# A four-layer decoder on one core: the exponential and the context matmuls of three sixteen-head attentions in two halves, with part of a projection between them

## The chip, the cores and the metric

The kernel runs on one core of a Trainium2 chip, as one launch. The metric is the device time in microseconds (us). The time before is 2404.22 us, the median of three runs (2397.91 to 2418.76).

## What is computed

`reference.py` is a decoder of four layers over 16 sequences of 128 tokens with 256 features. Every layer has an attention, a cross-attention and a feed-forward part, each followed by a residual sum and a layer norm. Three of these twelve sublayers have sixteen heads of 16 features each, and only they are changed: the cross-attention of layer 0 (`l0_xattn`), the attention inside the feed-forward part of layer 0 (`l0_ffn_attention`) and the cross-attention of layer 2 (`l2_xattn`). The last of them is, cut:

```python
q = split_heads(query @ Wq + bq)          # 16 heads of 16
k = split_heads(key @ Wk + bk)
v = split_heads(value @ Wv + bv)
scores = einsum('bhqd,bhkd->bhqk', q, k) / sqrt(16)
attn = softmax(scores, axis=-1)
ctx = einsum('bhqk,bhkd->bhqd', attn, v)
return merge_heads(ctx) @ Wo + bo
```

The first has a ReLU on q, k and v and no output projection. The second attends over the batch axis for each token position, so that a mask is laid over the scores ("masked" below).

## The kernel before

All twelve sublayers run one after the other, with a barrier of all engines behind each. The three attentions share the class `Heads16`. It makes 16 steps, one for each sequence, and a few behind them. PSUM is used as eight banks of 512 float32 columns.

A step k of `run_pe`, which fixes the order of TensorE's work, is this:

- `scores` of sequence k into banks 0 to 3: 16 matmuls (each two instructions, since float32 takes two) with 32 rows of the array each, four side by side as row tiles. VectorE then takes the maximum of each query and head out of them (L576, one `reduce_max` over 128x2048).
- `context` of sequence k-1 into bank 4 (L499): 16 matmuls, each 32 columns of the array wide, four side by side as column tiles. It waits for `exp_ready`, the exponential of sequence k-1.
- the `pieces(k)`: projections (`project` L170, `project_tokens` L179) and transposes that the next group of four sequences or the output needs. A piece fills one of the banks 5, 6, 7, in turn over all pieces (`bank`), and is copied out by ScalarE (q, k: L297, two instructions a piece) or VectorE (v, y). `keep_running` (L110) puts a few idle matmuls there in some steps that have no piece.
- four transposes of the negated maxima into bank 0 (L512), which wait for VectorE's L576; VectorE adds them to q (L586).
- four transposes of the context of sequence k-1 into bank 1 (L521); VectorE divides by the sum (L592, L594).
- `shifted` scores of sequence k, keys by queries, into banks 4 to 7, so they wait until the context and all pieces have been copied out. They wait for L586.

ScalarE's step copies the context out of bank 4 (L546), takes its pieces, and makes the exponential of banks 4 to 7 in one instruction of 128x2048 (L556) into `probs`, `[128, 4, 4, 128]` by row group r and round t. So context k-1 lies between `scores` k and the pieces of k, and starts when the whole exponential is done, while every later use of banks 4 to 7 needs the same. Head h = 4t + r sits in row group r, which is bank 4 + r of `shifted`, and in column group r of the context. The host lays the weights out in that order (`slots`, `side_by_side`).

The pieces of a step go by its place in a group of four: two x, two k, ("turned" x only from the third group on); two c, one q; two y, one q; two v, two h. `l0_xattn` has k, q and v alone. The steps for the last group have no k, q, v of a next one.

## Time and profile before

| | |
|---|---|
| runs, median (lowest to highest) | 2404.22 us (2397.91 to 2418.76) |
| the profiled execution | 2399.57 us |
| its span, first to last instruction | 2397.8 us |
| mean granted clock of TensorE | 0.939 |
| `l0_xattn`, first to last exponential | 214.3 to 350.2 us |
| `l0_ffn_attention`, the same | 402.5 to 550.4 us |
| `l2_xattn`, the same | 1288.9 to 1422.1 us |
| exponentials L556 in all | 48 of 1877 ns |

In the profile, PE is TensorE's matmuls, PEld its weight loads, DVE is VectorE, ACT ScalarE, POOL GpSimd. A row of the timeline is: start in us, duration in us, engine, line, operation, output<-inputs, shape, count; in square brackets stands how long the engine had been idle before it and what it waited for. Consecutive instructions of one kind are merged into one row.

### The profile page before, as it was taken

What the parts mean: (1) busy time and instruction counts of PE and PEld (TensorE: products, weight loads), DVE (VectorE), ACT (ScalarE), POOL (GpSimd) and SP (SyncE); (2) the same over time, 40 slices, a digit from 0 to 9 for tenths busy, and PEclk for the clock granted to TensorE, in tenths of its full rate; (3) what the DMA queues carried; (4) which work ended last, traced back from release to release, by engine and by line L of the source; (5) the groups of instructions that cost most, each with busy time, mean ns of one, the idle gap of its engine ahead of it and who ended that gap; (6) DMA issues with size and microseconds to landing.
All of it is one profiled execution on the core that took longest, in us unless ns stands there. A gap on an engine that the chain in (4) does not pass through costs nothing. (4 is left out here: it accounts for less than half of the span.)

```text
span 2397.8 us, 37176 instructions
## 1 busy us (share of the span) xinstructions
PE 2017.7 (84%) x14090; PEld 1441.2 (60%) x14107; DVE 1440.8 (60%) x2869; ACT 935.7 (39%) x1542; POOL 784.6 (33%) x555
## 2 busy tenths in 40 slices
PE   6998765883996796599877879998998989789998
PEld 5775553662895585599535655684343434355887
DVE  3885884567233567211474564235799999999333
ACT  3433423430111344233334421113675666655443
POOL 1221231225002111100313014005688798978200
PEclk9999987996898887799988999999999999999999
DMA  5217001002996110799100003492210110200000
GB/s 169 80 41 268 19 23 50 2 19 71 336 382 231 46 36 18 275 357 380 47 1 28 2 2 131 124 269 85 80 42 30 36 35 25 95 9 1 10 10 18
DMA packets 104721, 232.65 MB, mean 97 GB/s; under 512 B 10016, under 2 KB 77472, under 8 KB 95584
## 3 DMA queue, kind: packets, MB, share of 16 engines
q1 hardware_dynamic: 95808, 208.24, 24.7%
q0 software_dynamic: 7680, 20.98, 2.7%
q8 instruction: 114, 1.87, 0.3%
q10 hardware_dynamic: 1056, 1.05, 0.1%
q14 instruction: 63, 0.52, 0.1%
HBM read 174.27 MB, written 55.97 MB: 96 GB/s over the span
## 5 line engine op out<-in xcount | busy, mean ns | idle before, releaser
L4273 POOL TENSOR_TENSOR l_attn_ring<-l_attn_ring,l_attn_c_rows 128x1024 f32<-128x1024 f32 x128 | 301.7, 2357 | 77.2 <-DVE l_attn_ring L4085 77.2
L4085 DVE TENSOR_TENSOR_SCAN l_attn_ring<-bank,l_attn_ring 128x512 f32<-128x512 f32 x256 | 299.2, 1210 | 21.5 <-ACT bank L3889 17.0
L3645 PE MATMUL bank<-l_attn_ring,identity 128*128 128x512 f32 x512 | 244.8, 600 | 17.2 <-POOL l_attn_ring L4273 13.9
L3889 ACT ACTIVATE bank<-l_attn_step,l_attn_minus_exp_a_log 128x508 f32<-128x508 f32 x256 | 173.8, 685 | 156.7 <-DVE l_attn_ring L4085 155.9
L170 PE MATMUL bank<-x_features,weights 128*128 128x512 f32 x416 | 199.2, 618 | 14.8 <-ACT l_attn_silu_z L3803 4.9
L3645 PEld LDWEIGHTS bank<-l_attn_ring,identity 128*128 128x128 f32 x512 | 95.5, 192 | 124.4 <-issue 98.0
L4079 DVE TENSOR_TENSOR l_attn_ring<-l_attn_step_times_input,bank 128x1024 f32<-128x1024 f32 x128 | 153.4, 1198 | 1.8 <-issue 1.3
L576 DVE TENSOR_REDUCE negmax_slots<-bank 128x16 f32<-128x2048 f32 x48 | 109.8, 2288 | 60.7 <-PE bank L462 60.3
L170 PEld LDWEIGHTS bank<-x_features,weights 128*128 128x128 f32 x416 | 79.0, 196 | 106.2 <-issue 87.4
L179 PE MATMUL bank<-weights,x_features 128*128 128x256 f32 (+1 forms) x336 | 99.7, 452 | 8.1 <-ACT weights L3919 3.3
L556 ACT ACTIVATE l_xattn_probs<-bank 128x2048 f32<-128x2048 f32 x32 | 60.1, 1877 | 102.2 <-PE bank L462 102.2
L1874 ACT ACTIVATE l_attn_hidden<-bank,l_attn_tile_weights 128x128 f32<-128x128 f32 x176 | 50.2, 368 | 110.9 <-PE bank L170 110.9
L179 PEld LDWEIGHTS bank<-weights,x_features 128*128 128x128 f32 x336 | 66.4, 202 | 37.0 <-issue 23.4
L170 PE MATMUL bank<-l_attn_tile_xT,l_attn_tile_weights 128*128 128x128 f32 x704 | 83.9, 278 | 3.5 <-DMA l_attn_tile_weights<-l_ffn_experts 3.5
L170 PEld LDWEIGHTS bank<-l_attn_tile_xT,l_attn_tile_weights 128*128 128x128 f32 x704 | 83.6, 195 | 4.7 <-issue 3.6
L179 PE MATMUL bank<-l_attn_tile_weights,l_attn_hidden 128*128 128x256 f32 x352 | 79.5, 379 | 0.0
L170 PEld LDWEIGHTS bank<-l_ffn_experts_tile_xT,ffn_experts_tile_weights 128*128 128x128 f32 x592 | 71.7, 192 | 3.6 <-issue 1.8
L1878 ACT ACTIVATE l_ffn_experts_hidden<-bank 128x512 f32<-128x512 f32 x39 | 23.3, 597 | 129.4 <-PE bank L170 129.4
L170 PE MATMUL bank<-l_ffn_experts_tile_xT,ffn_experts_tile_weights 128*128 128x128 f32 x592 | 72.3, 275 | 0.9 <-issue 0.9
L289 POOL TENSOR_SCALAR x_tokens<-x_tokens,l_xattn_x_mean_var,l_xattn_x_rstd 128x256 f32<-128x256 f32 x24 | 34.1, 1427 | 115.5 <-DVEq L285 115.5
L3956 ACT ACTIVATE weights<-bank,weights 128x512 f32<-128x512 f32 x64 | 45.6, 713 | 63.0 <-PE bank L3699 61.7
L179 PEld LDWEIGHTS bank<-l_attn_tile_weights,l_attn_hidden 128*128 128x128 f32 x352 | 65.2, 190 | 8.0
(750 smaller groups left out, 4417.2 us busy)
## 6 DMA issues: line engine op xcount, KB each, us to landing
l_attn_tile_weights<-l_ffn_experts SPq DMA_DIRECT2D x22, 2180.0 KB, 9.7
ffn_experts_tile_weights<-l_ffn_experts_experts SPq DMA_DIRECT2D x37, 1024.0 KB, 8.2
expert_slots<-zeros SPq DMA_DIRECT2D x8, 2048.0 KB, 11.6
l_attn_c_rows<-state_outputs SPq DMA_DIRECT2D x64, 256.0 KB, 3.3
l_ffn_tile_weights<-l_ffn_experts SPq DMA_DIRECT2D x23, 512.0 KB, 4.7
expert_slots<-residual_sum SPq DMA_DIRECT2D x62, 128.0 KB, 8.4
expert_slots<-zeros SPq DMA_DIRECT2D x1, 5888.0 KB, 27.8
l_ffn_tile_x<-expert_slots SPq DMA_DIRECT2D x23, 256.0 KB, 4.3
```

Of the source, the lines that this page charges most:

```text
L170: mm = pe.matmul(out, w[:, f, m * P:(m + 1) * P], src[:, f, :], start=start and f == 0, stop=stop and f == k - 1)
L179: mm = pe.matmul(out, srcT[:, f, seq(b)], w[:, f, :], start=start and f == 0, stop=stop and f == k - 1)
L289: engine.tensor_scalar(out, src, self.mv[:, n, 0:1], self.rstd[:, n:n + 1], ALU.subtract, ALU.mult).then_inc(done, 1)
L556: nc.scalar.activation(self.probs[k % 2][:].rearrange("p r t q -> p r (t q)"), self.shifted, ACT.Exp, scale=self.scale).then_inc(self.exp_ ...
L576: nc.vector.reduce_max(slots[:, :, SHIFT_ROW].rearrange("p (t r) -> p r t", t=4), self.scores.rearrange("p r (t k) -> p r t k", t=4), AX_X ...
L1874: ins = net.nc.scalar.activation(self.hidden[t % 2][:, m, :], bank[:, i * self.tile:(i + 1) * self.tile], self.func, bias=self.b1(t, m))
L3645: mm = pe.matmul(net.banks[SUMS[j]][:], net.ident[:], ring[n % 4][:, j, :], start=s == 0, stop=s == STATES - 1)
L3889: nc.scalar.activation(by_seq(net.banks[DECAY[j]][:])[:, :, 1:], by_seq(dt[:, m, :])[:, :, 1:], ACT.Exp, scale=a[:, m * STATES + s:m * STA ...
L3956: nc.scalar.activation(full[n % 3], out[:], ACT.Relu, scale=by).then_inc(full_ready, 1)
L4079: tt(ring[n % 4][:], dtu[:, 2 * half_:2 * half_ + 2, :], net.banks[B_ROW[n % 2]][:].unsqueeze(1).broadcast_to([P, 2, T]), ALU.mult).then_i ...
L4085: nc.vector.tensor_tensor_scan(ring[n % 4][:, j, :], net.banks[DECAY[j]][:], ring[n % 4][:, j, :], 0.0, ALU.mult, ALU.add).then_inc(state_ ...
L4273: tt(ring[n % 4][:], ring[n % 4][:], c_row[:, n % STATES, :].unsqueeze(1).broadcast_to([P, 2, T]), ALU.mult).then_inc(out_ready, 1)
```

## The change

- `run_act` makes the exponential of a step with two instructions of 128x1024, the first over banks 4 and 5, the second over banks 6 and 7. Each counts up `exp_ready`.
- `run_pe` makes the context in two halves of eight heads (`context_half`), the first when the first exponential is done, the second when the second is. Both use all four column groups. For that the heads are laid out anew, by the host (`by_place`): heads 8c to 8c+7 lie in the row groups 2c and 2c+1.
- Between the halves stands what `between(k)` names: of a first piece k, q, v or y its first part (`project`: the first of two blocks of the contraction, `project_tokens`: the first of two sequences); of a first piece h, x or c the whole of it; nothing where there is none. The rest comes behind the second half.
- A step's pieces now take the banks 5, 6, 7 from bank 5 on in each step (`side`), so the first piece is in a bank that the first exponential has read. `last_there` names the piece that was in the same bank before.

Of the diff, the new signatures of `work` in `l0_ffn_attention` and `l2_xattn` are left out; they pass `parts` on as that of `l0_xattn` does.

```diff
--- before.py
+++ after.py
@@ -163,10 +163,10 @@
                 mm.then_inc(done, 1)
 
 
-def project(pe, out, w, src, m, start=True, stop=True):
+def project(pe, out, w, src, m, start=True, stop=True, of=None):
 
     k = w.shape[1]
-    for f in range(k):
+    for f in range(k) if of is None else of:
         mm = pe.matmul(out, w[:, f, m * P:(m + 1) * P], src[:, f, :], start=start and f == 0,
                        stop=stop and f == k - 1)
     return mm
@@ -388,6 +388,7 @@
 
     SIDE = (5, 6, 7)
     STEPS = SEQUENCES + 5
+    IN_PARTS, TURNED = "kqvy", "hxc"
 
     def __init__(self, net, sub, signals, masked, scale, first, pieces, by_act, steps=STEPS, fill={}, ahead=None):
         self.STEPS, self.ahead = steps, ahead
@@ -399,6 +400,10 @@
         order = list(first) + [p for k in range(self.STEPS) for p in pieces(k)]
         self.by_act = by_act
         self.number = {p: n for n, p in enumerate(order)}
+        self.side = {p: self.SIDE[i % 3] for ps in [list(first)] + [pieces(k) for k in range(self.STEPS)]
+                     for i, p in enumerate(ps)}
+        self.last_there = {p: max([m for m in range(n) if self.side[order[m]] == self.side[p]], default=-1)
+                           for n, p in enumerate(order)}
         self.act_upto, self.dve_upto = [], []
         for p in order:
             self.act_upto.append((self.act_upto or [0])[-1] + by_act(p))
@@ -438,7 +443,7 @@
         return slots_act(self.net, to, src, func, u, own, bias)
 
     def bank(self, name):
-        return self.net.banks[self.SIDE[self.number[name] % 3]]
+        return self.net.banks[self.side[name]]
 
     def wait_taken(self, engine, n):
 
@@ -464,15 +469,32 @@
                                skip_group_check=True, tile_position=(at, 0))
         return mm
 
+    def between(self, k):
+
+        names = self.pieces(k)
+        if names and names[0][0] in self.IN_PARTS:
+            return [(names[0], (1,))] + [(name, (0, 1)) for name in names[1:]], [(names[0], (0,))]
+        ahead = 1 if names and names[0][0] in self.TURNED else 0
+        return [(name, (0, 1)) for name in names[ahead:]], [(name, (0, 1)) for name in names[:ahead]]
+
     def run_pe(self, pe, work):
         net, done = self.net, 0
 
-        def do(name):
-            n = self.number[name]
-            if n >= 3:
-                self.wait_taken(pe, n - 3)
-            net.keep_running(pe, self.bank(name), self.fill.get(name, 0))
-            work(self.bank(name), *name).then_inc(self.filled, 1)
+        def do(name, parts=(0, 1)):
+            if 0 in parts:
+                self.wait_taken(pe, self.last_there[name])
+            mm = work(self.bank(name), *name, parts)
+            if 1 in parts:
+                mm.then_inc(self.filled, 1)
+
+        def context_half(n, c):
+            pe.wait_ge(self.exp_ready, 2 * n + c + 1)
+            for h in range(8 * c, 8 * c + 8):
+                at, t, r = SLOT * (h % 4), 2 * (h // 4 % 2) + h // 2 % 2, 2 * c + h % 2
+                mm = pe.matmul(self.ctxT[at:at + SLOT, seq(h // 4)], self.v1(n // NB, n % NB)[:, h, :],
+                               self.probs[n % 2][:, r, t, :], start=True, stop=True,
+                               skip_group_check=True, tile_position=(0, at))
+            return mm
 
         for name in self.first:
             do(name)
@@ -490,19 +512,18 @@
                                    net.mates_q, net.mates_k).then_inc(self.scores_ready, 1)
             if 1 <= k <= SEQUENCES:
                 n = k - 1
-                pe.wait_ge(self.exp_ready, n + 1)
                 if n % NB == 0 and ("v", n // NB, 1) in self.number:
                     self.wait_taken(pe, self.number["v", n // NB, 1])
-                for t in range(4):
-                    for r in range(4):
-                        at = SLOT * r
-                        mm = pe.matmul(self.ctxT[at:at + SLOT, seq(t)], self.v1(n // NB, n % NB)[:, 4 * t + r, :],
-                                       self.probs[n % 2][:, r, t, :], start=True, stop=True,
-                                       skip_group_check=True, tile_position=(0, at))
-                mm.then_inc(self.contextT_ready, 1)
-            for name in self.pieces(k):
-                do(name)
-                done += 1
+                context_half(n, 0)
+                behind, between = self.between(k)
+                for name, parts in between:
+                    do(name, parts)
+                context_half(n, 1).then_inc(self.contextT_ready, 1)
+            else:
+                behind = [(name, (0, 1)) for name in self.pieces(k)]
+            for name, parts in behind:
+                do(name, parts)
+            done += len(self.pieces(k))
             if ("max", k) in self.fill:
                 self.wait_taken(pe, done - 1)
                 net.keep_running(pe, net.banks[7], self.fill["max", k])
@@ -553,8 +574,9 @@
                 act.wait_ge(self.shifted_ready, k + 1)
                 if k >= 2:
                     act.wait_ge(self.contextT_ready, k - 1)
-                nc.scalar.activation(self.probs[k % 2][:].rearrange("p r t q -> p r (t q)"), self.shifted,
-                                     ACT.Exp, scale=self.scale).then_inc(self.exp_ready, 1)
+                for of in (slice(0, 2), slice(2, 4)):
+                    nc.scalar.activation(self.probs[k % 2][:, of, :, :].rearrange("p r t q -> p r (t q)"),
+                                         self.shifted[:, of, :], ACT.Exp, scale=self.scale).then_inc(self.exp_ready, 1)
 
     def run_dve(self, dve, chain, take, rest, between=None):
         net, nc = self.net, self.net.nc
@@ -1157,12 +1179,12 @@
             def _(pe):
                 pe.wait_ge(net.ready["l0_xattn"], 16)
 
-                def work(out, kind, g, i):
+                def work(out, kind, g, i, parts):
                     if kind == "k":
-                        return project(pe, out, wk, net.ctxT_all[:, g, :, :], i)
+                        return project(pe, out, wk, net.ctxT_all[:, g, :, :], i, of=parts)
                     if kind == "q":
-                        return project(pe, out, wq, net.xT_all[:, g, :, :], i)
-                    for b in (2 * i, 2 * i + 1):
+                        return project(pe, out, wq, net.xT_all[:, g, :, :], i, of=parts)
+                    for b in (2 * i + part for part in parts):
                         mm = project_tokens(pe, out[:, (b % 2) * D:(b % 2 + 1) * D], net.ctxT_all[:, g, :, :], b, wv)
                     return mm
 
...
@@ -1285,9 +1307,9 @@
                     if kind == "k":
                         if i == 0:
                             heads.wait_taken(pe, heads.number["h", g, 1])
-                        return project(pe, out, wk, xT, i)
+                        return project(pe, out, wk, xT, i, of=parts)
                     if kind == "q":
-                        return project(pe, out, wq, xT, i)
+                        return project(pe, out, wq, xT, i, of=parts)
                     if kind == "logits":
                         if g == 0:
                             pe.wait_ge(net.ready["l0_ffn_experts"], 16)
@@ -1300,7 +1322,7 @@
                         return route.count_pe(pe, out, of_group(g))
                     if kind == "y" and i == 0:
                         heads.wait_taken(pe, heads.number["c", g, 1])
-                    for b in (2 * i, 2 * i + 1):
+                    for b in (2 * i + part for part in parts):
                         to = out[:, (b % 2) * D:(b % 2 + 1) * D]
                         mm = project_tokens(pe, to, cT, b, wo) if kind == "y" else project_tokens(pe, to, xT, b, wv)
                     return mm
...
@@ -3038,12 +3060,12 @@
                         pe.wait_ge(heads.context_ready, NB * (g + 1))
                         return turn(out, heads.context, i)
                     if kind == "k":
-                        return project(pe, out, wk, net.ctxT_all[:, g, :, :], i)
+                        return project(pe, out, wk, net.ctxT_all[:, g, :, :], i, of=parts)
                     if kind == "q":
-                        return project(pe, out, wq, net.xT_all[:, g, :, :], i)
+                        return project(pe, out, wq, net.xT_all[:, g, :, :], i, of=parts)
                     if kind == "y" and i == 0:
                         heads.wait_taken(pe, heads.number["c", g, 1])
-                    for b in (2 * i, 2 * i + 1):
+                    for b in (2 * i + part for part in parts):
                         to = out[:, (b % 2) * D:(b % 2 + 1) * D]
                         if kind == "y":
                             mm = project_tokens(pe, to, cT, b, wo)
@@ -4614,9 +4636,17 @@
     return v.reshape(-1, P).T
 
 
+def by_place(a):
+
+    import numpy as np
+    heads = np.arange(NH).reshape(2, 2, 2, 2).transpose(1, 2, 0, 3).reshape(-1)
+    return a.reshape(*a.shape[:-1], NH, DH)[..., heads, :].reshape(a.shape)
+
+
 def slots(a, row=0.0):
 
     import numpy as np
+    a = by_place(a)
     out = np.zeros((*a.shape[:-1], 2, 2, 4, SLOT), a.dtype)
     heads = a.reshape(*a.shape[:-1], 2, 2, 4, DH)
     out[..., 0, :, 0:DH], out[..., 0, :, SHIFT_ROW] = heads[..., 0, :, :], row
@@ -4627,7 +4657,7 @@
 def side_by_side(a):
 
     import numpy as np
-    heads = a.reshape(*a.shape[:-1], 2, 2, 4, DH)
+    heads = by_place(a).reshape(*a.shape[:-1], 2, 2, 4, DH)
     return np.ascontiguousarray(np.swapaxes(heads, -3, -2)).reshape(*a.shape[:-1], D)
 
 
```

## Rows read from the trace of the kernel before

**Rows 1.** The page, busy time of each engine
```profile
PE 2017.7 (84%) x14090; PEld 1441.2 (60%) x14107; DVE 1440.8 (60%) x2869; ACT 935.7 (39%) x1542; POOL 784.6 (33%) x555
```

**Rows 2.** Who waited for whom, PE alone, of `l0_xattn`, `l0_ffn_attention`, `l2_xattn` (total us, times, longest)
```profile
PE bank L499 <- ACT l_xattn_probs L556: 16.4, 16, 2.0
PE bank L512 <- DVE negmax_slots L576: 8.2, 5, 2.1
...
PE bank L499 <- ACT l_ffn_attention_probs L556: 15.4, 16, 2.0
PE bank L512 <- DVE negmax_slots L576: 5.2, 1, 5.2
...
PE bank L499 <- ACT l_xattn_probs L556: 17.7, 16, 2.0
PE bank L512 <- DVE negmax_slots L576: 0.8, 2, 0.6
```

**Rows 3.** Timeline of one step of `l0_xattn` with two k pieces
```profile
238.93 1.07 PE L462 MATMUL bank<-l_xattn_k_slots,l_xattn_q_slots 32*128 32x128 f32 x32
239.17 1.88 ACT L556 ACTIVATE l_xattn_probs<-bank 128x2048 f32<-128x2048 f32 x1 [5.08 <-PE bank L462]
241.10 1.08 PE L499 MATMUL bank<-l_xattn_probs,values_and_one 128*32 128x128 f32 x32 [1.10 <-ACT l_xattn_probs L556]
242.11 3.70 PE L170 MATMUL bank<-ctx_features,weights 128*128 128x512 f32 x8
242.87 2.27 DVE L576 TENSOR_REDUCE negmax_slots<-bank 128x16 f32<-128x2048 f32 x1
245.65 0.60 PE L512 MATMUL bank<-identity,negmax_slots 128*128 128x128 f32 x4
247.64 1.17 PE L462 MATMUL bank<-l_xattn_q_slots,l_xattn_k_slots 32*128 32x128 f32 x32 [0.96 <-ACT l_xattn_k_slots L297]
```

**Rows 4.** Groups of instructions on ACT, each shape apart (busy us, mean ns)
```profile
L556 ACT ACTIVATE l_xattn_probs<-bank 128x2048 f32<-128x2048 f32 x32 | 60.1, 1877 | 102.2 <-PE bank L462 102.2
L1878 ACT ACTIVATE l_ffn_experts_hidden<-bank 128x512 f32<-128x512 f32 x39 | 23.3, 597 | 129.4 <-PE bank L170 129.4
L2378 ACT ACTIVATE l_attn_gate<-x_tokens 128x1024 f32<-128x1024 f32 x4 | 4.2, 1057 | 0.1
```

**Rows 5.** Timeline of another stage: whole-array transposes, then row tiles
```profile
74.57 0.60 PE L958 MATMUL bank<-identity,residual_sum 128*128 128x128 f32 x4
...
75.10 1.15 PE L926 MATMUL bank<-l_attn_qk,weights 32*128 32x256 f32 x16
```

**Rows 6.** Timeline: a masked step with one q piece, and the wait for the exponential
```profile
404.49 2.29 DVE L576 TENSOR_REDUCE negmax_slots<-bank 128x16 f32<-128x2048 f32 x1
407.27 0.60 PE L512 MATMUL bank<-identity,negmax_slots 128*128 128x128 f32 x4
...
513.02 1.08 PE L499 MATMUL bank<-l_ffn_attention_probs,values_and_one 128*32 128x128 f32 x32 [0.90 <-ACT l_ffn_attention_probs L556]
```

**Rows 7.** Timeline of a step of `l0_xattn` that waits for VectorE (PE, then DVE)
```profile
263.46 0.66 PE L512 MATMUL bank<-identity,negmax_slots 128*128 128x128 f32 x4 [1.86 <-DVE negmax_slots L576]
264.90 2.09 PE L462 MATMUL bank<-l_xattn_q_slots,l_xattn_k_slots 32*128 32x128 f32 x32 [0.34 <-DVE l_xattn_q_slots L586]
...
261.12 2.29 DVE L576 TENSOR_REDUCE negmax_slots<-bank 128x16 f32<-128x2048 f32 x1
```

**Rows 8.** Timeline of the last step of `l0_xattn`
```profile
348.35 1.88 ACT L556 ACTIVATE l_xattn_probs<-bank 128x2048 f32<-128x2048 f32 x1 [4.42 <-PE bank L462]
350.28 1.93 PE L499 MATMUL bank<-l_xattn_probs,l_xattn_values_and_one 128*32 128x128 f32 x32 [2.00 <-ACT l_xattn_probs L556]
```

**Rows 9.** Busy time and granted clock of the three stages (us busy, counts, PEclk, DMA share)
```profile
214.30:354.00 139.70, 106.00 (x1709) 79.81 (x1707) 117.02 (x161) 54.36 (x55) 39.16 (x28) 0.94 0.23 79
402.50:552.00 149.50, 119.91 (x1927) 93.06 (x1920) 94.82 (x203) 58.56 (x61) 43.86 (x33) 0.97 0.03 9
1288.90:1424.00 135.10, 106.66 (x1759) 83.34 (x1752) 73.49 (x129) 56.05 (x56) 15.76 (x13) 0.98 0.01 2
```

4 lines of the change are left out of this document (2 added, 2 removed).

## The prediction

> **What bounds the kernel now.** I read the page first: TensorE is busy for 84% of the span, the other engines for 60% or less [rows 1]. So TensorE's idle time is what a change of order can win, and only in the three stages that it touches. They last some 140, 150 and 135 us [rows 9], 425 of 2398 us.
>
> Next the waits of TensorE in these stages. The context matmuls (L499) wait for the exponential (L556) 16 times in each, 16.4, 15.4 and 17.7 us in all: 49.5 us, or 1.03 us at each of 48 steps. The maxima's transposes (L512) wait for VectorE's reduction (L576) 8 times, 14.2 us in all [rows 2].
>
> Then the timeline of a step. `scores` end at 238.93 + 1.07 = 240.00. The exponential started at 239.17 and ends at 241.05, and the context starts at 241.10. Between them TensorE has nothing, for 1.10 us [rows 3]. In the masked stage the mask's matmuls fill 0.2 us of it, and 0.9 is left [rows 6]. From there pieces, transposes and the `shifted` scores follow without a wait that doesn't move with the pieces: the last take of a piece, or L586, ends 1 us after the transposes start. So the chain of a step is exponential, context, pieces, transposes, L586 or L297, `shifted`, exponential. It has a second strand, `scores` to L576 to the transposes.
>
> **The change, part by part.**
>
> *The exponential in two.* Not in the trace is a 128x1024 one from PSUM. Of the same engine 128x512 from PSUM takes 597 ns and 128x2048 takes 1877 [rows 4], that is 0.833 ns per column. So 1024 columns take 597 + 427 = 1024 ns. The 1057 ns of a 128x1024 with its input in SBUF is near it. The second half ends at 2.05 us after the start, 0.17 later than now. That costs nothing while TensorE works on a piece until then.
>
> *The first context half* can start 1.02 + 0.05 = 1.07 us after the start of the exponential, not 1.93. `scores` have ended by then (0.83; masked 1.04, so perhaps 0.03 later). So 0.86 us of the idle time goes.
>
> *TensorE's work is the same, but the form of the matmuls changes twice more in a step*: column tiles, whole array, column tiles, whole array, where there was one such change. From tiles to the whole array: the 32 context instructions start 0.026 us apart ((1.08 - 0.27) / 31, each lasting 0.27), so they need 0.84, and the projection starts 1.01 after them: 0.17. Its 8 instructions then take 3.54 until the transposes, against 8 x 0.43 = 3.44: 0.10 more [rows 3]. Together 0.27. From the whole array to tiles I have only the row tiles of another stage: four transposes 0.109 apart should be through at 75.01, and the tiles start at 75.10: 0.09 [rows 5]. So the two extra changes cost 0.36 us. The lower bound is 0, if the weight loads go ahead beside the running matmuls. The upper is 0.62, if both changes also expose the whole of a load and of a last matmul's tail (0.11 + 0.16, 0.19 + 0.16 from the durations in the same rows). I take 0.36, because the rows show these very changes or the nearest ones.
>
> The Trainium skill speaks against this edit ("TensorEngine Tiling (Array Packing)", Key Properties): to change the tiling mode drains TensorE. It gives no price. Its page "TensorE: Matmul & The Clock Gate" (Single matmul latency) has 398 cycles beside the columns for a matmul that nothing overlaps. By that a drain would be 166 ns at 2.4 GHz, two of them 0.33, and the sum 1 us better than mine.
>
> *What a step gains*: 0.86 - 0.36 = 0.50 us, if there is work for between the halves and the second half isn't reached early. First half and change last 0.42 + 0.27, part of a k, q, v or y piece 0.86 (two instructions of 0.43, or four of 0.22), a whole x, c or h piece 0.44. So the second half is reached 2.2 us after the start at the earliest, behind the second exponential's 2.10.
>
> *Where it is lost.* A step whose transposes wait for L576 gains nothing. They do so at 8 steps [rows 2], at one of which the reduction starts only at 261.12, behind VectorE's layer norm, and TensorE stands for 1.86 us [rows 7]. Going through all 48 steps, I find three more that are held in this way or another: by the reduction's end within 0.1 us, by VectorE's two takes of v behind a late reduction, and by `scores` that run at half clock. These 11 are steps 5, 9 and 11 to 14 of `l0_xattn` (counting from 0), 10 and 14 of `l0_ffn_attention`, 0, 2 and 14 of `l2_xattn` (its 0 is the one with the slow `scores`). In the last step of each stage there is no new sequence. The other 34 have a slack of 0.4 us or more. One of the tightest is the q step where L576 ends at 406.78 and the transposes start at 407.27 [rows 6]; it loses nothing, since ScalarE's take of q ends later than L586 there.
>
> *The last steps.* Here the context runs at half clock, 1.93 us after a wait of 2.00 [rows 8]. With halves of 0.97 the first runs beside the second exponential, and the second ends at 2.10 + 0.97 = 3.07 after the start, not at 3.86. That is 0.8 us in `l0_xattn`, and perhaps 0.5 and 0.6 in the two stages where an x piece stands between: 1.9 us.
>
> *Banks, copies, the other queues.* The first piece goes into bank 5 in every step, but all pieces were already waited for ahead of `shifted`, so no wait is added. The context's copy (L546) comes some 0.3 us later or at the same time as now; it is followed by takes that come 0.5 earlier and still start after it. No DMA is added or moved; SP's and POOL's queues keep their order. Behind the stages the barriers pass every gain on.
>
> *The sum*: 34 x 0.50 + 1.9 = 18.9 us, 19. Against the profiled execution's own time, 2399.6, that is 2380.6. The median of the runs is 4.6 us above that execution, and I set the gain against the median: 2404.2 - 19 = **2385 us**, 0.8% faster. With 0.62 for the changes it is 34 x 0.24 + 1.9 = 10, or 2394. With 0 it is 34 x 0.86 + 1.9 = 31, less some 3 where the slack is below 0.86: 28, or 2376.
>
> **The rivals.**
>
> *The changes of form are hidden*: 2376. For it: TensorE loads weights ahead in long streams. Against it: the gap of 0.17 behind each context.
>
> *VectorE takes over in more steps.* L576 needs 2.29 us each time and VectorE is busy for 117 of 140 us in `l0_xattn` [rows 9]. A step that gets shorter brings its norms and sums nearer to the next reduction. In the 9 steps of that stage that I count on, half of the gain may go, and as much in the masked stage if the routing joins in: 9 us less, 2394. Against it: the slack that I found in each step.
>
> *The gain is given back at the ends of the stages*, say because weights that are being fetched arrive no earlier: 2404. Against it: DMA is nearly idle in two of the stages [rows 9].
>
> *Slower: the clock.* The mean granted clock is 0.94 to 0.98 in the stages [rows 9], and the half clock (1.2 of 2.4 GHz) shows around the steps where TensorE waits for VectorE: behind the 1.86 us of idleness `scores` take 2.09 us, not 1.17 [rows 7]. The change turns the short wait for the exponential into a longer one for L576 in just these 11 steps. A whole step at half clock costs 0.9 for each of three groups of tiles and 1.7 for a q piece, some 4 us. From 5 such steps on the gain is gone. If all 11 get there, it is 44 - 19 = 25 us slower: 2429. Against it: the idle time of a whole step stays the same or gets less.
>
> **How the numbers follow.** The forecast 0.57 (its own range 2378 to 2392), hidden changes 0.13, VectorE 0.15, given back 0.07, slower 0.08. The range reaches from 5 us below 2376 to just above 2404, 2371 to 2405, and leaves out the slower case and a little on both sides. A change of less than 1% (24 us) can't be told from none here, since the three runs of before lie 21 us apart; 1% faster is below 2380.2. By the cases: 0.12 of the hidden changes and 0.2 of the forecast make 0.32 faster; slower by over 1% is the clock's 0.08; the rest, 0.60, is within 1%.
>
> **What would show it.** In the profile after: L556 96 times at 1.02 us; the first context half 1.07 us after the first exponential, with an idle time of 0.2 before it; the second half with no wait for the exponential in 34 steps, and 0.2 to 0.3 us between its last instruction and the projection. The sum of TensorE's waits on L556 falls from 49 us to some 12. The three stages get shorter by 5.3, 7.0 and 6.6 us. The waits of L512 on L576 grow from 14 us to some 20. I'm wrong about the changes of form if a step with a q piece gets shorter by 0.2 or by 0.8 rather than 0.5; wrong about VectorE if L512 waits at more than 12 steps; wrong about the clock if a stage's granted clock falls below 0.9.

## The result, and the profile after

The changed kernel takes 2389.45 us (median of 12 runs, 2379.76 to 2397.83), the kernel before in the same session 2407.88 (12 runs, 2397.91 to 2418.76): a ratio of 0.9924, with an interval of 0.9906 to 0.9943. In a later session it was 2393.33 against 2403.75: 0.9946 [0.9924, 0.9968]. So it is 0.5 to 0.8% faster, 13 to 18 us by the ratios and 10 to 18 by the medians. 2385 was predicted, 19 less than the median known then; that median rose by 3.7 us with more runs. Of the first kernel under "The experiments" one run took 4230.23 us, the nine others 2412.56 to 2424.67; its ratio leaves that run out.

The profiled execution of after takes 2390.27 us (span 2388.5), the one of before 2399.57. Its busy line, beside [rows 1]:

```profile
PE 2038.9 (85%) x14090; PEld 1438.0 (60%) x14107; DVE 1441.8 (60%) x2869; ACT 938.4 (39%) x1590; POOL 783.7 (33%) x555
```

The same 14090 matmuls, and 48 more instructions on ScalarE: the second exponentials. The groups of the exponentials (busy us, mean ns), beside [rows 4]:

```profile
L578 ACT ACTIVATE l_xattn_probs<-bank 128x1024 f32<-128x1024 f32 x64 | 62.1, 1021 | 97.9 <-PE bank L467 97.9
```

1021 ns each; 1024 was worked out. TensorE's waits in `l0_xattn`, `l0_ffn_attention` and `l2_xattn` (total us, times, longest), beside [rows 2]; L494 is the context, L578 the exponential, L533 the maxima's transposes, L598 the reduction:

```profile
PE bank L533 <- DVE negmax_slots L598: 10.8, 6, 2.6
PE bank L494 <- ACT l_xattn_probs L578: 5.7, 18, 1.1
...
PE bank L533 <- DVE negmax_slots L598: 5.8, 1, 5.8
...
PE bank L494 <- ACT l_ffn_attention_probs L578: 1.4, 2, 1.2
...
PE bank L494 <- ACT l_xattn_probs L578: 5.3, 17, 1.1
...
PE bank L533 <- DVE negmax_slots L598: 1.6, 2, 1.0
```

The waits for the exponential fell from 49.5 to 12.4 us (12 predicted), those for the reduction rose from 14.2 to 18.2 (20 predicted), at 9 places rather than 8. The step of [rows 3] is now this (start, duration):

```profile
236.62 1.94 ACT L578 ACTIVATE l_xattn_probs<-bank 128x1024 f32<-128x1024 f32 x2 [4.22 <-PE bank L467]
237.69 0.64 PE L494 MATMUL bank<-l_xattn_probs,values_and_one 128*32 128x128 f32 x16 [0.25 <-ACT l_xattn_probs L578]
238.27 1.12 PE L170 MATMUL bank<-ctx_features,weights 128*128 128x512 f32 x2
239.32 0.64 PE L494 MATMUL bank<-l_xattn_probs,values_and_one 128*32 128x128 f32 x16
239.90 2.84 PE L170 MATMUL bank<-ctx_features,weights 128*128 128x512 f32 x6
240.31 2.28 DVE L598 TENSOR_REDUCE negmax_slots<-bank 128x16 f32<-128x2048 f32 x1
242.64 0.66 PE L533 MATMUL bank<-identity,negmax_slots 128*128 128x128 f32 x4
244.48 1.17 PE L467 MATMUL bank<-l_xattn_q_slots,l_xattn_k_slots 32*128 32x128 f32 x32 [0.74 <-ACT l_xattn_k_slots L297]
```

The first half starts 1.07 us after the exponential, as predicted, where the whole context started at 1.93. The idle time before it is 0.25, not 1.10. The second half waits for nothing. The transposes start 6.02 after the exponential (6.48 before) and `shifted` 7.86 after it (8.47 before). The reduction ends at 242.59 here, so it is VectorE that sets the transposes' 242.64, and by 0.1 us at most (in the third kernel below, with no such wait, they start 2.68 after the same six matmuls do; here it is 2.74).

The steps of this kernel repeat so exactly that they measure better than the total. I call a step the time from one (first) exponential to the next. In two executions of before the 34 steps that the prediction counted on agree to 0.01 us on the mean. Here they are, with the rest of the span beside them (us; "three last steps" is the sum over the stages of the time from the last step's first exponential to its context's transposes):

```
                                     before   before   after    after    after
                                              again             again    timed
34 steps, against before                  -      0.0   -17.0    -16.4    -16.4
the 11 other steps                     99.7     98.2    98.3    100.8    101.3
three last steps, exponential to
  the context's transposes             14.6     13.7    10.5     11.0     11.0
last exponential of l0_ffn_attention
  to the first of l2_xattn            740.4    736.7   750.8    738.0    756.9
span                                 2397.8   2397.2  2388.5   2379.8   2397.2
```

The 34 steps gained 0.48 to 0.50 us each. The fourth line, a stretch that the change doesn't touch, lies between 737 and 757 us. In the profiled execution of after it took back 10.5 of the 22.5 us that the first three lines had gained, and the rest of the span another 2.7, so the spans are only 9.3 apart.

### The profile page after: what moved, and what is told of

Same layout as the page of the kernel before. It is cut to its first block and busy times, and to the rows that moved or that the text cites. A ratio compares the mean times of both kernels' runs of the same rounds, so it can differ in the third digit from the quotient of the medians.

```text
span 2388.5 us, 37231 instructions
## 1 busy us (share of the span) xinstructions
PE 2038.9 (85%) x14090; PEld 1438.0 (60%) x14107; DVE 1441.8 (60%) x2869; ACT 938.4 (39%) x1590; POOL 783.7 (33%) x555
## 5 line engine op out<-in xcount | busy, mean ns | idle before, releaser
L170 PE MATMUL bank<-x_features,weights 128*128 128x512 f32 x416 | 204.5, 627 | 17.0 <-ACT l_attn_silu_z L3825 4.9
L598 DVE TENSOR_REDUCE negmax_slots<-bank 128x16 f32<-128x2048 f32 x48 | 109.8, 2287 | 59.6 <-PE bank L467 59.1
L578 ACT ACTIVATE l_xattn_probs<-bank 128x1024 f32<-128x1024 f32 x64 | 62.1, 1021 | 97.9 <-PE bank L467 97.9
```

Source lines behind the costliest of these rows:

```text
L170: mm = pe.matmul(out, w[:, f, m * P:(m + 1) * P], src[:, f, :], start=start and f == 0, stop=stop and f == k - 1)
L578: nc.scalar.activation(self.probs[k % 2][:, of, :, :].rearrange("p r t q -> p r (t q)"), self.shifted[:, of, :], ACT.Exp, scale=self.scale ...
L598: nc.vector.reduce_max(slots[:, :, SHIFT_ROW].rearrange("p (t r) -> p r t", t=4), self.scores.rearrange("p r (t k) -> p r t k", t=4), AX_X ...
```

## The experiments

**Taking the change apart.** Three kernels, and the one with a whole piece between that follows them, were compared with the kernel before at 2412.37 us (median). After each measured time stand its ratio to the kernel before with the 95% interval, and the mean change of the 34 steps against before. The first has the two exponentials and two halves of the context, but both halves wait for the second exponential, and nothing stands between them:

```diff
-            pe.wait_ge(self.exp_ready, 2 * n + c + 1)
+            pe.wait_ge(self.exp_ready, 2 * n + 2)
...
-                behind, between = self.between(k)
+                behind, between = [(name, (0, 1)) for name in self.pieces(k)], []
```

> The changed kernel with the exponential still in two instructions, but the whole context behind both of them and nothing between its halves. What is left of the change is the second instruction's fixed cost and the new places of heads and banks. Mine: the context starts 2.10 us after the first exponential instead of 1.93, so a step that TensorE's chain sets is 0.17 us longer than before: 34 such steps make 6 us, ratio to the kernel before 1.002 to 1.003. Rival, the extra ACT instruction is free or the new places gain something: step lengths as before or shorter, ratio 1.000 or less. A loss of over 0.3 us a step would mean that the two instructions cost more than the rows of before made likely.

Measured: 2415.39 us (median of all ten runs), 1.0016 [0.9993, 1.0039]; 0.085 a step (0.06 in most, 0.15 in every fourth). The same step:

```profile
241.16 1.94 ACT L578 ACTIVATE l_xattn_probs<-bank 128x1024 f32<-128x1024 f32 x2 [5.08 <-PE bank L467]
243.15 1.08 PE L494 MATMUL bank<-l_xattn_probs,values_and_one 128*32 128x128 f32 x32 [1.16 <-ACT l_xattn_probs L578]
244.16 3.70 PE L170 MATMUL bank<-ctx_features,weights 128*128 128x512 f32 x8
...
247.70 0.60 PE L533 MATMUL bank<-identity,negmax_slots 128*128 128x128 f32 x4
```

The context starts 1.99 after the first exponential, not 2.10. Two exponentials of 1.02 are through in 1.94: the second starts 0.92 after the first, before the first has ended. So to split the exponential costs 0.06 (1.99 against 1.93), not 0.17. This kernel also has the new places of the heads and the new banks, so these gain nothing by themselves: no step is shorter, and the 0.06 is that of the context's later start. The 0.15 is looked at under "A wait in another place".

The second has only the change of `between` to nothing (the second line pair above): halves that wait for their own exponential, and no piece between.

> The changed kernel with each context half started as soon as its own exponential is done, but no piece between them: TensorE waits there. No extra change of form with work on both sides. Mine: first half at 1.08 us, second at 2.10 us after the first exponential, the first piece at 2.10 + 0.44 + 0.17 = 2.71 instead of 2.94: each of 34 steps 0.23 us shorter than before, 8 us, and 2 us from the three last steps, ratio 0.996. If the changes of form were free (rival), the changed kernel would gain 0.86 a step and this one still 0.23; so the difference between this and the changed kernel is 0.27 a step by mine and 0.63 by the rival, 9 us or 21 us.

Measured: 2392.5 us, 0.9916 [0.9888, 0.9943]; -0.38 a step (0.23 was expected).

```profile
237.54 1.94 ACT L578 ACTIVATE l_xattn_probs<-bank 128x1024 f32<-128x1024 f32 x2 [5.08 <-PE bank L467]
238.62 0.64 PE L494 MATMUL bank<-l_xattn_probs,values_and_one 128*32 128x128 f32 x16 [0.25 <-ACT l_xattn_probs L578]
239.53 0.65 PE L494 MATMUL bank<-l_xattn_probs,values_and_one 128*32 128x128 f32 x16 [0.27 <-ACT l_xattn_probs L578]
240.11 3.70 PE L170 MATMUL bank<-ctx_features,weights 128*128 128x512 f32 x8
```

The first half runs beside the second exponential, the second half starts at 1.99, and the projection 2.57 after the exponential (2.94 before [rows 3]). So three quarters of the step's gain come from the halves alone. The part of a projection between them adds 0.12 a step (0.27 was expected), 4 us in 34: it brings 0.86 us of work forward, but the second half starts 0.71 later for it, at 2.70 against 1.99. The timed runs don't show this part of the gain: the ratios of this kernel and of after are 0.9916 and 0.9924.

The third has the part between the halves, but both halves wait for the second exponential (the first line pair). Against the first kernel it differs by the two changes of form alone:

> The changed kernel with the part of a piece between the context halves kept, but both halves behind the second exponential: all of the two extra changes of form and none of the earlier start. Mine: 0.17 for the second exponential plus 0.36 for the two changes make each of the 34 steps 0.53 us longer than before and 0.36 longer than with the halves late and no part between; 18 us slower than before, ratio 1.0075. Rival, changes of form are free: 0.17 a step, 6 us, ratio 1.0025, no difference to the kernel with the halves late and no part.

Measured: 2426.32 us, 1.0062 [1.0031, 1.0094]; +0.40 a step (0.53 was expected, with 0.17 of it for the second exponential).

```profile
247.34 0.64 PE L494 MATMUL bank<-l_xattn_probs,values_and_one 128*32 128x128 f32 x16 [1.16 <-ACT l_xattn_probs L578]
247.91 1.13 PE L170 MATMUL bank<-ctx_features,weights 128*128 128x512 f32 x2
248.97 0.64 PE L494 MATMUL bank<-l_xattn_probs,values_and_one 128*32 128x128 f32 x16
249.54 2.84 PE L170 MATMUL bank<-ctx_features,weights 128*128 128x512 f32 x6
...
252.22 0.49 PE L533 MATMUL bank<-identity,negmax_slots 128*128 128x128 f32 x3
```

From the context's start to the transposes it is 252.22 - 247.34 = 4.88 us, against 247.70 - 243.15 = 4.55 in the first kernel: 0.33 for the two extra changes, where 0.36 was predicted. On the mean of the 34 steps it is 0.31 (0.34 where the part is of a k, q, v or y piece, 0.28 where it is an x or c piece). The rows show where it lies: 2 matmuls of 0.43 each take 1.06 from their start to the next half (0.20 more), and each half takes 0.57, where half of 1.01 would be 0.50. That settles the rival of hidden changes: they aren't hidden. The Trainium skill's rule ("TensorEngine Tiling (Array Packing)", Key Properties) that a change of mode drains the engine agrees with this; whether the 0.33 is a drain or weight loads that stand exposed, these rows don't tell. My estimate of 0.33 from the latency that the Trainium skill gives for a bf16 matmul ("TensorE: Matmul & The Clock Gate", Single matmul latency) was nearer than my own 0.36.

**A whole piece between.** Where a k, q, v or y piece comes first, all of it stands between the halves:

```diff
-            return [(names[0], (1,))] + [(name, (0, 1)) for name in names[1:]], [(names[0], (0,))]
+            return [(name, (0, 1)) for name in names[1:]], [(names[0], (0, 1))]
```

> The changed kernel with the whole first piece k, q, v or y between the context halves, not its first part. Same number of changes of form, twice the work between. Mine: TensorE's order costs the same, so v and y steps keep their length. But the context's copy ends 0.86 us later, at about 4.9 us, and ScalarE takes a lone q piece only behind it: steps with only a q piece get some 0.45 us longer and those with two k pieces some 0.15, in all 3 to 4 us slower than the changed kernel, ratio to before 0.993 to 0.995. Rival, the size of the part doesn't matter: every step as in the changed kernel. Rival, a larger part hides more: shorter steps, below 0.992.

Measured: 2390.97 us, 0.9899 [0.9839, 0.9959]. Steps with more than one piece are as long as in after (I had expected those with two k pieces to lose), but for one of `l0_xattn` that ran at half clock; a step whose only piece is q is 0.32 to 0.35 us longer than in after (0.45 expected). One of these:

```profile
250.41 1.94 ACT L578 ACTIVATE l_xattn_probs<-bank 128x1024 f32<-128x1024 f32 x2 [1.49 <-PE bank L467]
251.57 0.64 PE L494 MATMUL bank<-l_xattn_probs,l_xattn_values_and_one 128*32 128x128 f32 x16 [0.33 <-ACT l_xattn_probs L578]
252.15 1.98 PE L170 MATMUL bank<-x_features,weights 128*128 128x512 f32 x4
...
254.77 0.58 ACT L567 COPY l_xattn_context_slots<-bank 128x512 f32<-128x512 f32 x1 [2.43 <-PE bank L494]
255.25 1.27 ACT L297 ACTIVATE l_xattn_q_slots<-bank,weights 128x512 f32<-128x512 f32 x2
256.78 1.17 PE L467 MATMUL bank<-l_xattn_q_slots,l_xattn_k_slots 32*128 32x128 f32 x32 [0.71 <-ACT l_xattn_q_slots L297]
```

The context ends late, so its copy (254.77) does, ScalarE's takes of q queue behind the copy, and `shifted` waits for them. The seven q steps make 2.3 us together, for which the smaller part is the better one; the two totals can't be told apart (four runs of this kernel lie 23 us apart).

**Each kernel once more.** One further execution of before and one of after, to see what belongs to the kernels and what to the execution:

> The kernel before once more, for its trace. The time between the last exponential of l0_ffn_attention and the first of l2_xattn, stages that the change doesn't touch, was 740.35 us in the trace of before and 750.84 in that of the changed kernel. If that is chance, from one execution to the next, this trace may have anything from 740 to 753 there. If the change brings it about, it is 740 again, within 1 us. The three changed stages should last 134.0, 146.0 and 131.3 us again, each within 1.

> The changed kernel once more, for its trace. Same question as with the kernel before: by chance the untouched stretch lies anywhere from 740 to 753 us; by the change it is 751 again. The three changed stages should last 127.9, 140.0 and 125.1 us again, each within 1.

Measured: 2399.03 and 2381.64 us. The step lengths were given above: 34 steps the same to 0.02 us on the mean, the rest not. The stage `l0_xattn` was expected the same within 1 us and wasn't: 132.1 against 134.0 in before, 131.7 against 127.9 in after. The untouched stretch fell outside what I gave for either case: 736.7 and 738.0. After was also timed once more with its profile:

> The changed kernel once more, timed beside the two that follow. Mine: ratio to the kernel before 0.992, as on record, within 0.002. The sum of its 34 steps is 17 us below before's; where the trace's total differs from before's by another amount than some 19 us, it is the untouched stretch between l0_ffn_attention and l2_xattn, which has been 736.7 and 740.4 in two traces of before and 738.0 and 750.8 in two of this kernel.

Measured: 2393.33 us, 0.9946 [0.9924, 0.9968], a little off the 0.992 within 0.002 that I expected. The two later executions of after, one program with equal steps, are 17.4 us apart in span, and the untouched stretch 18.9; they come from different sessions and chips. The part of it where they come apart, cut at the same instructions of VectorE in both (length, busy times, granted clock, DMA share, GB/s), in the shorter and then the longer execution:

```profile
783.20:983.60 200.40, 135.65 (x941) 114.89 (x940) 123.18 (x457) 69.85 (x130) 30.77 (x32) 0.82 0.21 73
```

```profile
786.00:1003.90 217.90, 150.28 (x938) 127.27 (x936) 123.47 (x457) 70.05 (x128) 30.91 (x32) 0.76 0.20 70
```

The same work takes 17.5 us longer there, nearly all of the difference, and its granted clock is 0.76, not 0.82. An attention of another kind stands there. A group of its matmuls (busy us, mean ns), in the same order:

```profile
L2250 PE MATMUL bank<-l_attn_unit_qkT 64*128 64x128 f32 x256 | 18.6, 285 | 0.0
```

```profile
L2250 PE MATMUL bank<-l_attn_unit_qkT 64*128 64x128 f32 x256 | 23.1, 332 | 0.0
```

The same 256 matmuls are at half clock for more of the time. Over all thirteen executions the stretch lies between 737 and 757 us; both of before are at the short end (737, 740), the eleven others have a mean of 747. It seems to go by the session more than by the kernel: the four executions of one session, with the second of before (736.7) and the second of after (738.0), lie between 737 and 745, the three of the last session between 748 and 757. Whether changed kernels come upon a worse clock there more often isn't settled by two executions of before; the timed runs below speak against a large effect.

**A wait in another place.** In every fourth step of the first kernel and of after the context starts 0.09 us late. There TensorE waits for the take of a v piece in an instruction of its own, ahead of the context. Here the two waits change places:

```diff
+            if c == 0 and n % NB == 0 and ("v", n // NB, 1) in self.number:
+                self.wait_taken(pe, self.number["v", n // NB, 1])
             for h in range(8 * c, 8 * c + 8):
...
-                if n % NB == 0 and ("v", n // NB, 1) in self.number:
-                    self.wait_taken(pe, self.number["v", n // NB, 1])
                 context_half(n, 0)
```

> The changed kernel with one wait moved. Every fourth step TensorE also waits until the values have been taken; the change put that wait ahead of the wait for the first exponential, where it stood behind it before. In these steps the first context half starts at 1.17 us after the exponential, in the others at 1.08. Mine: it is the order of the waits, and with the old order these steps start at 1.08 too: 8 steps that count get 0.09 us shorter, 0.7 us, which the times can't tell from the changed kernel (0.992), but the trace can. Rival: something else in these steps holds the context, and 1.17 stays.

Measured: 2383.28 us (the kernel before, timed beside it, 2407.69), 0.9894 [0.986, 0.9927]. The start of such a step in after, and then here:

```profile
245.71 1.94 ACT L578 ACTIVATE l_xattn_probs<-bank 128x1024 f32<-128x1024 f32 x2 [1.49 <-PE bank L467]
...
246.88 0.64 PE L494 MATMUL bank<-l_xattn_probs,l_xattn_values_and_one 128*32 128x128 f32 x16 [0.33 <-ACT l_xattn_probs L578]
```

```profile
248.42 1.94 ACT L578 ACTIVATE l_xattn_probs<-bank 128x1024 f32<-128x1024 f32 x2 [1.49 <-PE bank L467]
...
249.50 0.64 PE L496 MATMUL bank<-l_xattn_probs,l_xattn_values_and_one 128*32 128x128 f32 x16 [0.24 <-ACT l_xattn_probs L578]
```

(L496 is this kernel's context line.) 1.17 has become 1.08, and these steps are 0.09 to 0.10 shorter (7.19 against 7.29). With the late wait passed first, the wait for v, met long ago, costs nothing; the other way round it delays the start. (1.08 is the start in the steps without a wait for v, too.)

**Three exponentials.** With the previous edit, of one, one and two quarters; the context in parts of 4, 4 and 8 heads, the projection's part ahead of the last; the heads are reordered to match (L579 is its exponential, L496 its context):

```diff
-                for of in (slice(0, 2), slice(2, 4)):
+                for of in (slice(0, 1), slice(1, 2), slice(2, 4)):
...
-            for h in range(8 * c, 8 * c + 8):
-                at, t, r = SLOT * (h % 4), 2 * (h // 4 % 2) + h // 2 % 2, 2 * c + h % 2
+            for h in range(*((0, 4), (4, 8), (8, 16))[c]):
+                at, t, r = SLOT * (h % 4), h % 4, h // 4
```

> On top of the old order of waits: three exponentials, over banks 4, 5 and 6 to 7, and the context in parts of four, four and eight heads, with the piece's part behind the second. Mine: the first four heads start when scores end, at about 0.93, the next four when the second exponential is done, at 0.50 + 0.60 + 0.05 = 1.15, so the part of the piece starts 0.14 us earlier than in the changed kernel where there is no mask and 0.1 earlier in the masked stage. No change of form is added, the last exponential ends 0.06 later, which is hidden. 34 steps by 0.12 and 0.7 for the waits: 5 us faster than the changed kernel, ratio to before 0.990. Rival, each part costs TensorE another gap as a change of form does (0.3 us): 5 to 8 us slower than the changed kernel, ratio 0.995. Where the piece between is short (x, c, h) the last part may wait for its exponential until 2.07: 0.06 less there.

> The kernel with three exponentials again, timed beside the changed one. By the step lengths in its trace it is 5 us faster than the changed kernel (0.65 us a step below before, not 0.50): ratio to before 0.990, and 0.998 to the changed kernel. Rival: what the steps gain is lost elsewhere, and both have the same ratio.

Measured: 2385.65 us, 0.9916 [0.9884, 0.9949], and in the later session 2385.4, 0.9913 [0.9883, 0.9943] (0.990 expected; the kernel before 2403.75). The 34 steps are 0.65 and 0.63 shorter than before.

```profile
240.04 2.00 ACT L579 ACTIVATE l_xattn_probs<-bank 128x512 f32<-128x512 f32 x3 [4.22 <-PE bank L467]
240.79 0.81 PE L496 MATMUL bank<-l_xattn_probs,values_and_one 128*32 128x128 f32 x16
241.53 1.12 PE L170 MATMUL bank<-ctx_features,weights 128*128 128x512 f32 x2
```

The row of ACT names the form of the first of its three instructions; the third is of 1024 columns. The first context follows `scores` without a wait; the part starts 1.49 after the exponential, where it was 1.65 in after. That is 0.16, less what the third instruction adds; 0.11 was left on the mean against the previous kernel (0.12 expected), so the rival of one more gap of 0.3 us is out. It is 4 us in 34 steps, and the totals don't show that: in one session 2383.28 us without and 2385.65 with the third exponential. Both edits together show beside the changed kernel, timed in the later session: 2385.4 against 2393.33, and 10 of the changed kernel's 12 runs are above the slowest of these six.

**Idle matmuls where TensorE waits for VectorE.** To the last kernel, matmuls are added whose results nobody reads, ahead of the transposes that wait for the reduction (the kernel before had some in steps 12, 14 and 15 of `l0_xattn` and 15 of `l2_xattn`). A fill only waits for the banks to be taken where three pieces are in them:

```diff
-                      fill={("max", 12): 8, ("max", 14): 16, ("max", 15): 4})
+                      fill={("max", 6): 10, ("max", 10): 10, ("max", 12): 14, ("max", 13): 8, ("max", 14): 16,
+                            ("max", 15): 11})
...
+                        fill={("max", 15): 25})
...
-                        fill={("max", 15): 8}, ahead=net.ahead)
+                        fill={("max", 15): 11}, ahead=net.ahead)
```

> Three exponentials, and idle matmuls in the steps where TensorE waits for VectorE's maxima: 10 each in steps 5 and 9 of l0_xattn, 14, 8, 16 and 11 in its steps 11 to 14 (8, 0, 16 and 4 until now), 25 in step 14 of l0_ffn_attention (none), 11 in that of l2_xattn (8). What holds these steps is VectorE, but in some traces TensorE runs at half clock right behind the wait: step 9 lasted 9.67 us or 11.1, step 12 6.84, 8.1 or 8.7, with the same kernel. Mine: with the idle time filled the granted clock of l0_xattn is 1.0 throughout, step 9 takes 9.7, step 14 of l0_ffn_attention 11.3 to 11.6 instead of 12.3 to 12.7, and the three last contexts run at full clock; 3 to 5 us faster than with three exponentials alone, ratio 0.988. Rival: the half clock comes from elsewhere or the fills delay the transposes; then the same or slower.

Measured: 2378.91 us, 0.9892 [0.9857, 0.9927]. One such step, `l0_xattn`'s step 9, in the second execution of after, then in its first, and then with the fill:

```profile
296.10 1.11 PE L533 MATMUL bank<-identity,negmax_slots 128*128 128x128 f32 x4 [2.59 <-DVE negmax_slots L598]
...
298.00 2.09 PE L467 MATMUL bank<-l_xattn_q_slots,l_xattn_k_slots 32*128 32x128 f32 x32
```

```profile
295.66 0.66 PE L533 MATMUL bank<-identity,negmax_slots 128*128 128x128 f32 x4 [2.59 <-DVE negmax_slots L598]
```

```profile
293.31 2.32 PE L110 MATMUL bank<-strangers_of_q,identity_bf 128*128 128x512 bf16 x10
296.54 0.66 PE L535 MATMUL bank<-identity,negmax_slots 128*128 128x128 f32 x4 [0.91 <-DVE negmax_slots L600]
...
297.98 1.17 PE L467 MATMUL bank<-l_xattn_q_slots,l_xattn_k_slots 32*128 32x128 f32 x32 [0.34 <-DVE l_xattn_q_slots L610]
```

After 2.59 us of idle time the transposes and `shifted` run at half clock in the first of these (1.11, 2.09) and at full clock in the second, where the step is 9.67 us, after the same idle time; behind the fill they run at full clock (0.66, 1.17). The step is 10.00 us with it, not 11.05 (9.7 had been expected). So this step doesn't show what a fill does. Step 14 of `l0_ffn_attention` does. Its transposes, with the fill ahead of them:

```profile
529.99 0.66 PE L535 MATMUL bank<-identity,negmax_slots 128*128 128x128 f32 x4 [0.24 <-DVE negmax_slots L600]
```

In the twelve executions without this fill, of all kernels, TensorE was idle for 4.8 to 5.8 us there, the four transposes then took 1.11 or 1.12 us, and the step 12.0 to 12.8; here it takes 11.24, a little less than the 11.3 to 11.6 expected. The stage's granted clock, from its first to its last exponential, is 1.00 here and 0.97 or 0.98 in the twelve. That of `l0_xattn` is 1.00 too, as I had expected, against 0.96 and 0.94 with three exponentials alone; but the third kernel had 1.00 there without the added fills. The three last contexts run at full clock. Against three exponentials alone the 11 steps are 4.6 us shorter (96.7 against 101.3, the mean of two executions), the 34 steps 0.03 each. That is one execution, and the totals (2378.91 against 2385.4 in the same session) have overlapping intervals. This is the best kernel that was run: 14 us below the changed one in the same session, by medians (2378.91, 2393.33), of which the fills alone are 6.5; the intervals of the two ratios just overlap.

## Why the prediction was right

The time fell by 18.4 us in the first session, 19 were predicted; in the later one by 10.4, or 13 by the ratio. So that the first came within 1 us is in part luck. The steps say more surely what a kernel gains, and the timed runs should agree. The first three columns are the profiled execution's (the mean where there are several), against the mean of the two of before; the last is (ratio - 1) x 2408:

```
                               34 steps  11 steps  last 3   sum   timed runs
after, three executions          -16.6      +1.2     -3.4   -18.8  -18, -13
first (late halves, no part)      +2.9      +0.2      0.0    +3.1   +4
second (halves, no part)         -12.9      +1.4     -2.7   -14.2  -20
third (late halves, part)        +13.6      +0.9     +2.2   +16.7  +15
whole piece between              -14.3      +1.2     -1.8   -14.9  -24
waits in the other order         -18.2      +0.1     -3.7   -21.8  -26
three exponentials (twice)       -21.8      +2.3     -3.1   -22.5  -20, -21
with fills                       -22.7      -2.2     -3.9   -28.9  -26
```

The intervals of the timed runs are 9 to 17 us wide, that of the whole piece 29. All ten but that one lie within 6 us of their sum. So no large part of the gain is lost outside the steps, though a few us can't be ruled out: both timings of after show less than its sum.

*The gain of a step* was predicted as 0.86 - 0.36 = 0.50 us; it was 0.50, and 0.48 in two more executions. The idle time that goes was right (1.10 to 0.25). The changes of form cost 0.33, and the choice of the nearest rows over the bounds of 0 and 0.62 held. So the mechanism was right here; the halves and the two changes of form were each measured apart. Every fourth step has 0.42 for 0.51 because of the order of two waits, which I had not seen, though the code shows it.

*The second exponential* was mis-sized: ready at 1.99, not 2.10, since the second instruction on ScalarE starts 0.10 before the first has ended. It cost nothing here, as TensorE reaches the second half only at 2.70 (2.2 where an x, c or h piece comes first). But it made my expectation for the second kernel too small, and with it the share of the gain that the halves have alone.

*The last steps* were the term most wrong: 3.4 us on the mean, not 1.9. (With them the stages of the profiled execution are shorter by 7.4, 7.2 and 7.9 us, where 5.3, 7.0 and 6.6 were predicted.) I had left the context at half clock, because it ran so behind 2.00 us of idle time [rows 8]. In the profiled execution of after it runs at full clock behind a shorter wait:

```profile
341.22 1.94 ACT L578 ACTIVATE l_xattn_probs<-bank 128x1024 f32<-128x1024 f32 x2 [4.80 <-PE bank L467]
342.30 0.64 PE L494 MATMUL bank<-l_xattn_probs,l_xattn_values_and_one 128*32 128x128 f32 x16 [1.14 <-ACT l_xattn_probs L578]
```

16 matmuls take 0.64, half of the full-clock 1.08 and a little over, where 32 took 1.93. But the shorter wait isn't the whole reason. The same step in the second execution of before, and in the second of after:

```profile
351.77 1.08 PE L499 MATMUL bank<-l_xattn_probs,l_xattn_values_and_one 128*32 128x128 f32 x32 [2.00 <-ACT l_xattn_probs L556]
```

```profile
346.47 2.00 PE L494 MATMUL bank<-l_xattn_probs,l_xattn_values_and_one 128*32 128x128 f32 x32 [1.14 <-ACT l_xattn_probs L578]
```

Full clock behind 2.00 us, half clock behind 1.14. Over all executions the last context ran at half clock in 8 of 12 cases with a wait of 2.0 us or more (before, the first and the third kernel), and in 5 of 18 with one of 1.1 to 1.2 (after, the second kernel, the whole piece, the other order of waits). So half clock got rarer with the shorter wait, but what decides it in one case stays open, and part of the 3.4 us is luck. With the context at half clock in both, the last step of `l0_xattn` reaches the transposes at 3.78 and not 4.57, the 0.8 us that I had worked out; at full clock in both, at 3.34 and not 3.72. In the third kernel, where the wait is near 2 us again, the last steps are as long as before or longer.

*The 11 steps without gain* were set at 0. Their sum against before is -0.6 to +2.4 us in the three executions of after (against the mean of before's two). The list held for the profiled execution; what the 11 have instead is a spread of their own of 3 us, most of it from whether the clock halves behind a wait for VectorE.

*The rivals.* Changes that are hidden: out, by the 0.33. VectorE in more steps: L533 waits 9 times in each of the three executions, where the line was drawn at 12, and in the profiled one each of the 34 steps is at least 0.35 us shorter. Given back at the ends of the stages: out for the first and the last. From the last exponential of `l0_xattn` to the first of `l0_ffn_attention` it is 54.2 and 52.9 us in before, 53.1, 53.5 and 53.7 in after; less the last step, 49.6 and 49.2 against 49.8, 49.7 and 49.9. From the last exponential of `l2_xattn` to the end it is 975 to 980 in all of them. For the stretch between the second and the third stage it rests on the timed runs alone. The clock: in the three stages of the profiled execution the granted clock is no lower than in [rows 9]:

```profile
213.30:348.00 134.70, 106.64 (x1712) 74.19 (x1707) 118.83 (x170) 55.37 (x71) 41.11 (x31) 0.97 0.26 86
394.00:538.00 144.00, 126.54 (x1946) 92.16 (x1938) 95.35 (x208) 59.58 (x78) 43.85 (x33) 0.98 0.03 9
1284.00:1414.00 130.00, 113.05 (x1790) 83.22 (x1786) 73.50 (x130) 57.50 (x74) 16.85 (x14) 0.98 0.01 2
```

Its mechanism is there: steps 9, 10 and 14 of `l0_xattn` were 1.4, 0.7 and 0.9 us longer in two of the three executions of after, step 10 among them, one of the 34. The stage's granted clock is 0.94 in these two, still above the line drawn at 0.9, and from its first to its last exponential it takes 131.7 us, against 134.0 and 132.1 in before, so it is only 0.4 to 2.3 us shorter, where the forecast had 4.5. But this costs 3 us, not 44.

## What to carry to other kernels

Where a long instruction of ScalarE stands alone between two stretches of TensorE, cut it in two, and let the work on the first half run beside the second; that alone gave three quarters of a step's gain, and work put between the halves has to be worth more than the two changes of tile form that it costs (0.33 us). Of two waits, put the one that ends last first (0.09 us a step here). And where the steps of a kernel repeat, measure the steps: they agree to 0.02 us where totals differ by 17, and they show a gain of 4 us that the timed runs don't. Before you put a change of TensorE's clock down to an edit, look at the same instructions in a second execution: here both levels came behind the same idle time.

## What the runs showed of the chip

- Two ACTIVATE instructions of 1021 ns, one behind the other, are through in 1.94 us, the second starting 0.92 after the first; two of 128x512 and one of 128x1024 are through in 2.00, one of 128x2048 in 1.88.
- Two more changes between column tiles of 128x32 and the whole array cost 0.33 us in this stream: 0.07 for each context half and 0.20 around the two matmuls between.
- A wait in an instruction of its own ahead of another wait delayed the start by 0.09 us, though it was met long before.
- One program had its clock halved more often in one execution than in another, on another chip, in the same places: 285 or 332 ns a matmul on the mean of one group, 200.4 or 217.9 us for the same part of the program.
- Behind one and the same idle time the clock was halved in one execution and not in another: after 2.59 us, 1.11 or 0.66 us for four transposes; after 2.00 us, 1.93 or 1.08 for 32 context matmuls.
- With idle matmuls in a wait of 4.8 to 5.8 us for VectorE the four transposes behind it ran at full clock in the one execution with them (0.66 us), and at half clock in the twelve without (1.11 or 1.12): the step took 11.24 us, not 12.0 to 12.8.
